# A ScalarE copy, a GpSimd normalisation and a new TensorE order in the first attention's step

## What is computed

```python
x = x + _L0_xattn_ref(_layernorm(x), ctx_512, Wq, Wkv_expand, Wout)   # causal, 16 heads of 16
x = x + _L0_ffn_ref(_layernorm(x), router_w, ...)                     # shared + top-1 of 8 experts
x = x + _L1_xattn_ref(_layernorm(x), ctx_512, Wq, w_kc_q, ...)        # latent attention, 1444 keys
x = x + _L1_ffn_ref(_layernorm(x), ...)                               # ternary weights

# _L0_xattn_ref
scores = jnp.einsum('bhqd,bhkd->bhqk', qh, kh) * inv_sqrt_d
scores = jnp.where(causal, scores, jnp.finfo(scores.dtype).min)
attn = jax.nn.softmax(scores, axis=-1)
out = jnp.einsum('bhqk,bhkd->bhqd', attn, vh)
return out.transpose(0, 2, 1, 3).reshape(b, sq, H) @ Wout.T
```

## Time and profile before

| | us |
|---|---|
| median of 3 runs | 858.13 |
| lowest and highest | 857.02 and 858.37 |
| the profiled execution, its own time | 860.25 |
| span of the profiled execution | 858.1 |
| TensorE busy | 803.7 |
| VectorE busy | 578.6 |
| ScalarE busy | 371.2 |
| GpSimd busy | 465.4 |

### The profile page before, as it was taken

One profiled execution on the slowest core, in us unless ns is written; L12 is line 12 of the kernel. 1 busy time (PEld: TensorE's weight loads), 2 busy tenths in 40 slices (PEclk: granted clock), 3 DMA queues, 4 the chain that ended last, 5 costly groups with the idle time before them and its releaser, 6 DMA issues.

```text
span 858.1 us, 15473 instructions
## 1 busy us (share of the span) xinstructions
PE 803.7 (94%) x5850; PEld 594.0 (69%) x5850; DVE 578.6 (67%) x1125; ACT 371.2 (43%) x797; POOL 465.4 (54%) x474
## 2 busy tenths in 40 slices
PE   8888999999987999999999999999999999999896
PEld 6667748989765676776676767766676667756445
DVE  4688553223687675778787787778778777786445
ACT  3466422222203545445444544544454454454431
POOL 3122157000503977687867767776876775558630
PEclk9999999999999999999999999999999999999988
DMA  8821237895101000000000100000100000000000
GB/s 305 262 113 51 70 124 300 304 338 212 51 1 37 1 11 18 11 11 20 11 1 12 29 6 10 24 11 1 33 12 1 11 7 11 11 7 10 14 3 10
DMA packets 21897, 53.04 MB, mean 62 GB/s; under 512 B 7482, under 2 KB 15940, under 8 KB 19392
## 3 DMA queue, kind: packets, MB, share of 16 engines
q1 hardware_dynamic: 20800, 50.42, 17.2%
q0 software_dynamic: 1024, 1.64, 0.7%
HBM read 45.80 MB, written 5.36 MB: 60 GB/s over the span
## 4 chain that ended last, share of the span: by engine, by line
PE 71%; DVE 15%; issue 5%; ACT 4%; DMA 4%; SPq 1%; POOL 0%; POOLq 0%; ACTq 0%; DVEq 0%
PE ps L1163 15%; PE ps L1175 12%; PE ps L1143 7%; PE ps L1081 6%; PE ps L1025 3%; PE ps L1200 3%; PE ps L1086 3%; DMA xs<-xs_scratch 3%; PE ps L1109 3%; PE ps L1038 2%; PE ps L977 2%; DVE nm L1926 2%; DVE xyz L1897 2%; DVE sm L1712 1%; DVE xyz L1893 1%
## 5 line engine op out<-in xcount | busy, mean ns | idle before, releaser
L617 POOL TENSOR_TENSOR acc<-acc,pt 120x800 f32<-120x800 f32 (+1 forms) x157 | 299.0, 1904 | 93.3 <-ACT pt L1614 60.8
L1614 ACT ACTIVATE pt<-ps 120x400 f32<-120x400 f32 (+1 forms) x384 | 190.0, 505 | 226.2 <-PE ps L1163 215.7
L1926 DVE TENSOR_REDUCE nm<-ps 128x1 f32<-128x482 f32 (+1 forms) x336 | 213.6, 655 | 103.6 <-PE ps L1143 101.3
L1163 PE MATMUL ps<-qh,khl 128*120 128x400 f32 (+1 forms) x384 | 158.3, 412 | 10.2 <-ACT pt L1614 7.0
L1175 PE MATMUL ps<-pt,kv 120*64 120x400 f32 (+1 forms) x768 | 144.7, 513 | 0.0
L1143 PE MATMUL ps<-khl,qh 128*128 128x482 f32 (+1 forms) x336 | 131.1, 391 | 6.1 <-DVE nm L1926 5.2
L1163 PE MATMUL ps<-ql,kh 65*120 65x400 f32 (+1 forms) x384 | 134.3, 350 | 0.0
L1163 PEld LDWEIGHTS ps<-qh,khl 128*120 128x120 f32 (+1 forms) x384 | 70.8, 184 | 57.4 <-issue 31.0
L1175 PEld LDWEIGHTS ps<-pt,kv 120*64 120x64 f32 (+1 forms) x768 | 50.6, 138 | 65.1 <-issue 55.7
L1163 PEld LDWEIGHTS ps<-ql,kh 65*120 65x120 f32 (+1 forms) x384 | 71.2, 185 | 5.0
L617 POOL TENSOR_TENSOR acc<-pt,pt 121x800 f32<-121x800 f32 x16 | 30.6, 1912 | 74.8 <-ACT pt L1614 74.8
(11 more groups left out here) (259 smaller groups left out, 1207.7 us busy)
## 6 DMA issues: line engine op xcount, KB each, us to landing
ew<-in_expert_w_dram SPq DMA_DIRECT2D x14, 1536.0 KB, 7.4
fw<-in_ternary_w_dram SPq DMA_DIRECT2D x6, 512.0 KB, 7.6
spread<-inv_scratch SPq DMA_DIRECT2D x30, 100.0 KB, 2.7
craw<-in_ctx_dram SPq DMA_DIRECT2D x8, 360.0 KB
woT<-in_wo_t_dram SPq DMA_DIRECT2D x1, 2048.0 KB, 14.9
xs_scratch<-zero SPq DMA_DIRECT2D x1, 1792.0 KB, 8.7
xs<-xs_scratch SPq DMA_DIRECT2D x14, 128.0 KB, 7.2
ys_scratch<-ysb SPq DMA_DIRECT2D x14, 128.0 KB, 6.9
```

Of the source, the lines that this page charges most:

```text
L617: nc.gpsimd.tensor_tensor(total[r, :, :], before[r, :, :], pt[j % PT_BUF][r, :, :], ALU.add).then_inc(p_added, 1)
L1163: last = mm(ps[0:key_rows(t), k % 2, 0:HT], lhs[:, keys], rhs[:, HT * a:HT * a + HT], start=first, stop=not first)
L1614: nc.scalar.activation(pt[j % PT_BUF][0:rows, k % 2, :], ps[0:rows, k % 2, 0:HT], ACT.Exp).then_inc(p_ready, 1)
L1926: nc.vector.tensor_reduce(nm3[0:w, i, n:n + 1], ps[0:w, 3 + m % 2, 0:MN], AX.X, ALU.max).then_inc(m_reduced, 1)
```

## The change

It has four parts, all in the loop of the first attention.

1. TensorE: the scores of the next sequence stand directly behind `values0`, ahead of `turn_values0` and `out0`; they stood at the start of the next step. `turn_values0` now comes before `out0`.
2. TensorE: both `qb_head` products stand behind `turn_p0(b, 1)`; one of them stood ahead of it. ScalarE's `keep_p0(b, 1)` and `keep_qb(b)` swap places accordingly.
3. The copy `keep_values0` goes from VectorE to ScalarE, where it stands behind `keep_qb(b)` and ahead of `exponent0(b + 1)`.
4. The normalisation of x goes from VectorE to GpSimd, behind `power` of the same sequence. VectorE gets a wait for all eight before it multiplies them by the gate.

```diff
@@ gpsimd
                     power(rstd[:, b:b + 1], veps[:, b:b + 1], S).then_inc(rstd2_ready, 1)
+                    pool.wait_ge(rstd2_ready, b + 1)
+                    nc.gpsimd.tensor_scalar(xn[:, b, :], x_sb[:, b, :], mv[:, b, 0:1], rstd[:, b:b + 1],
+                                            ALU.subtract, ALU.mult).then_inc(xn2_ready, 1)
@@ tensor
+            def next_scores(b):
+
+                pe.wait_ge(s0_masked, b)
+                if b >= 2:
+                    pe.wait_ge(qb_kept_a, b - 1)
+                    pe.wait_ge(qb_kept_v, b - 1)
+                if b >= 3:
+                    pe.wait_ge(o0_kept, b - 2)
+                scores0(b)
+
-            for step in range(B + 4):
+            next_scores(1)
+            for step in range(1, B + 4):
...
-                if 1 <= step < B:
-                    pe.wait_ge(s0_masked, step)
...
-                    scores0(step)
...
-                if 1 <= step <= B:
+                if step <= B:
+                    turn_p0(step - 1, 1)
                     qb_head(2 * step - 2)
-                    turn_p0(step - 1, 1)
                     qb_head(2 * step - 1)
                     values0(step - 1)
+                    if step + 1 < B:
+                        next_scores(step + 1)
+                    turn_values0(step - 1)
                 if 2 <= step <= B + 1:
                     if step == B + 1:
                         keep_awake(0, SEAM[0])
                     out0(step - 2)
-                if 1 <= step <= B:
-                    turn_values0(step - 1)
@@ scalar
+            def keep_values0(b):
+
+                act.wait_ge(pv0_done, b + 1)
+                if b:
+                    act.wait_ge(v_turned, b)
+                keep(vT[:, :], ps[:, 6, 0:HT]).then_inc(vT_kept, 1)
...
                 if 1 <= step <= B:
+                    keep_p0(step - 1, 1)
                     keep_qb(step - 1)
-                    keep_p0(step - 1, 1)
+                    keep_values0(step - 1)
                 if 1 <= step < B:
                     exponent0(step)
@@ vector
-                    keep_values0(s - 1)
                     keep_qb(s - 1)
-                if s >= 3:
-                    norm_xn2(s - 3)
...
             dve.wait_ge(gate_ready, 1)
+            dve.wait_ge(xn2_ready, B)
```

More of the change, by code:

```diff
@@ L1748, in residual0 @@
                 ts(veps[:, b:b + 1], mv[:, b, 1:2], LN_EPS, None, ALU.add).then_inc(var2_ready, 1)
[L1750 to L1760, removed]
             def keep_qb(b):
```

## The result

The changed kernel is slower: 874.3 us (872.43 to 877.84, 4 runs) beside 858.25 for the kernel before, a ratio of 1.0186 with a 95% interval of 1.0158 to 1.0214, or +16.0 us. Forecast were 865.7 us and 861.7 to 870.0. The direction held, the forecast +7.6 is about half of the measured +16.0, and the time is outside the range. Run twice more beside other kernels, the same code gave 1.0115 (1.0065 to 1.0165) and 1.0145 (1.0107 to 1.0182), so +10 and +12 us; the mean of the three is +13. Ratios leave out executions more than 1.5% above the fastest of their kernel; medians do not.

The account below looks back on a forecast made before the run. No engine was full; each step was taken as a ring of dependences. Ring +4.2, GpSimd's normalisation and loop end +0.4, clock +3.0 gave +7.6 on the median 858.13: 865.7 us, range 861.7 to 870.0.

Parts of the forecast that it names:

- The ring through ScalarE: Loop: values, copy, nine exponentials, `xnT`, turns, `pT`, second turns, products; 8.69 us a step, 9.14 with logits; +4.2 us.
- the rival in which ScalarE's ring is slack and VectorE's decides: Loop: ScalarE reaches `keep_xn2` 0.8 to 1.2 us earlier, steps take 7.9 us; 857.2 to 857.6 us, chance 0.09.
- A sign that the forecast named: Profile after the change: VectorE waits before the masked add; no size given.
- The first two steps: Loop, sequences below 3: turns need only the first eight exponentials, so ScalarE's path takes 7.59 us a step.
- VectorE's ring: Loop: reciprocal to `veps`, `keep_qb`, scores, turn of the values; 7.9 us with or without logits, closed from the first residual.
- The early scores: TensorE in the loop: scores behind the values shorten the old ring, but VectorE's ring leaves the step no shorter.
- The 0.25 us wait of the copy: TensorE in the loop: both query-weight products behind the turns hide this wait for ScalarE's copy.
- GpSimd's normalisation: Hidden in the steps, on the path behind the last values: 0.66 us for VectorE's 0.405; term with output projection +0.4 us.
- The one-input case: Skill's rule that GpSimd is roughly line-rate with one input: normalisation near VectorE's time, term about 0.1 us.
- The clock: TensorE, five steps from sequence 3: idle of 1.3 and 0.9 us brings two falls to 1.2 GHz, 1.5 us each, +3.0.
- The discount from two rows in three: Clock term: three rows fell two times in three, but idle comes in two pieces, so two falls of five taken.
- the one with four or five falls: Rival: the ring closes and the clock falls in four or five steps; 868.7 to 870.2 us, chance 0.12.

Follow-up runs that it names:

- the kernel with `xnT` moved: The changed kernel with ScalarE's `keep_xn2` (the copy of the turned xn) placed between the first eight exponentials and the ninth: 865.61 us, ratio 1.0094.
- the filled one: The changed kernel with products nobody reads in every step's TensorE waits and six at the start of the shared part: 862.4 us, ratio 1.0032.

## Why the prediction was right or wrong

**The ring through ScalarE: right.** Forecast 8.69 and 9.14 us, found 8.79 and 9.07; forecast +4.2 for seven steps, found +4.4 (60.59 without a fall against 56.20). The kernel with the copy alone shows the same ring, and the kernel with `xnT` moved shows it 0.76 shorter. That also refutes the rival in which ScalarE's ring is slack and VectorE's decides: taking the ninth exponential out of ScalarE's path would then have changed nothing. A sign that the forecast named is there as well: in the steps at full clock VectorE waits 1.7 to 1.9 us ahead of `normalise0`, which comes just before the masked add.

**The first two steps: near in size, by another path.** Forecast 7.59, found 7.75. The forecast had them limited by ScalarE's eight exponentials, and VectorE's ring not yet closed. The chain shows VectorE's masked add in them: `turn_ao` waits for it, and the second turns stand behind `turn_ao`. That the lengths are so close is luck.

**The early scores: the place of the copy misread.** The forecast said that copy and normalisation, which leave VectorE, are not in VectorE's ring. Part 1 alone shows that while the copy is on VectorE, it is: the ring is 9.16 and not 7.9, and the step 1.2 us longer than in the kernel before. In the changed kernel, where the copy is gone from VectorE, this cost nothing, since ScalarE's ring decides there. The 0.25 us wait of the copy that the forecast saw hidden came back as 0.45 us ahead of the second turns when part 2 was tried by itself.

**GpSimd's normalisation: the place right, the size too small.** The forecast took 0.66 us from the line between two rows of other forms; it takes 1.23, inside the bounds of 0.457 and 1.523 and near the upper one. The line went through forms with one operation, and this one subtracts and multiplies in one instruction; whether the second operation is the reason wasn't tested. The price is +0.6 to +0.7 in place of +0.4. The one-input case of the Trainium skill (GPSIMD Engine Reference, section Engine selection), which the forecast set beside it, would have been further off: here the normalisation is three times VectorE's 0.405.

**The clock: the step that failed.** The forecast took two falls of 1.5 us each, +3.0, after one fall of the kernel before that lasted 3.4 us. Between the first values and the last logits the clock of the changed kernel was low for 20.5, 30.6 and 10.3 us in the three profiles, where two such falls make 6.8. It cost 7.9, 12.4 and 4.8 us there (what values and end of the loop took over the 60.59 and 9.19 us without a fall), 8.4 in the mean.

What was wrong is how often and how long the clock falls, and not what a short fall costs: the three of the third profile lasted 3.4 us each and added 1.59, 1.70 and 1.52. The second profile had six falls in that stretch, one of them in the first steps, for which the forecast had none. The first had two, the number forecast, but of 10.2 us each, over the turns, products, logits, values and scores; the second of them also slowed the end of the loop, 11.14 against 9.19 us. The discount from two rows in three, for idle that comes in two pieces, had no row behind it, and the waits are not the same in all five steps: 0.72 and 0.76 us in the first of them, 1.17 and 0.91 in the next, and only then 1.3 and 0.9.

With 4.4 for the loop, 0.65 for GpSimd and 8.4 for the clock the sum is 13.4, and the three measured values are 10, 12 and 16, 13 in the mean. The executions without a profile say the same. Over 63 of the kernel before, from the three sessions of the experiments, time and mean granted clock lie near a line: 848.8 us at full clock and 8.1 us more for each 0.01 below it, with a standard deviation of 1.2 us about it. The 16 of the changed kernel have a mean clock of 0.976 in place of 0.987. By the line that makes 9 us (an estimate, for the line goes down to 0.979 only), and they lie 3.8 us above the line; the filled one lies 4.5 above it. The four of the result had the lowest clock, 0.972, which makes 12 of their 16 us. Why it was lower in them than in the later ones stays open.

**The range.** Its upper end left out even five falls of 1.5 us (858.13 + 4.6 + 7.5 = 870.2). With five slowed steps at the measured 1.9 us, and 4.4 and 0.65, it would have been about 873, still under the measured 874.3: the sum had no term for falls in the first steps or the end of the loop. The nearest rival was the one with four or five falls, which had a chance of 0.12.

**The stretch behind the loop** was forecast to shift as a whole. It took 752.6 us before, from the last logits to the end of the span, and 751.0 after; over all profiles of this study it is between 747 and 754. That spread is as large as the ring's effect, and is why single executions say little here.

## What to carry to other kernels

A copy costs what is queued behind it: moving 0.5 us from a busy engine to an idle one closed a ring because it stood ahead of 3 us of exponentials that another engine needed. Before such a move, write the ring that it closes as a sum of starts to starts, and look where the freed work would be late next. A step that leaves TensorE more idle pays twice, once for the wait and once for the products after it at 1.2 GHz; price this as likely (11 of 15 steps were slowed here) and with long falls as well as short ones, and try filling the wait with products that nobody reads: in 33 loop steps whose waits were filled, in five kernels, none had a fall. A kernel whose steps already wait can be worth filling by itself: it gave half a percent here. And put the mean granted clock of every execution beside its time: it tells a lower clock from a longer path where only one execution has a profile.

## What the runs showed of the hardware

TensorE fell to 1.2 GHz behind waits of 1.3 and 0.9 us with only turns between them in many steps, but not in all: of three profiles of the same code one had all five steps slowed and two had three. One fall, at 64.7 us of the second profile, came behind waits of 0.64 and 0.69 us, while in the other two profiles waits of 0.7 and 0.8 at the same place passed without one. The clock stayed low for 3.4 us in some falls and for 6.8 or 10.2 in others. In the first long fall of the first profile TensorE was busy for all of the 6.8 us from 76.2 to 83.0 and stayed at 1.2 GHz. What decides between a short and a long fall stays open.

GpSimd took 1.23 us for a subtraction and multiplication of 100x256 float32 by two scalars a row, where VectorE takes 0.405; it took the same, within 0.02 us, in every kernel of this study that had it.
